# First layer's weighted sum: exponential steps waited for late, spread over all rows, and a new split into sets

## The reference

```python
for hd in range(4):
    h = inputs * W[hd]
    logits = (h @ a[hd, :D])[src] + (h @ a[hd, D:])[dst]
    e = exp(leaky_relu(logits, 0.2))              # one weight per edge and head
    rowsum = segment_sum(e, src, num_segments=N)
    agg = segment_sum(e[:, None] * h[dst], src, num_segments=N)
    outs.append(elu(agg / rowsum[:, None]))
return mean(outs)
```

## Time and profile before

| | us |
|---|---|
| median of 3 runs | 4653.99 |
| the three runs | 4649.1 to 4656.62 |
| span of the profiled execution | 4657.2 |
| the stretch of `sum_neighbours`, in the profile | about 1046 to 1733 |

### The profile page before, as it was taken

The page is one execution under the profiler, slowest core; times in us unless marked ns, Lnnn a source line. Parts: engine busy times, 40 slices in busy tenths (PEclk is TensorE's granted clock), DMA queues, the critical chain, the costliest instruction groups (busy, mean ns, idle before and its releaser), DMA issues. The chain is left out here.

```text
span 4657.2 us, 47765 instructions
## 1 busy us (share of the span) xinstructions
PE 1697.7 (36%) x10711; PEld 958.0 (21%) x10711; DVE 2833.9 (61%) x4928; ACT 1748.2 (38%) x4626; POOL 1878.2 (40%) x1844
## 2 busy tenths in 40 slices
PE   3162111100000000006666332322222179899989
PEld 2142111100000000001221110111111168444444
DVE  5837599873777779884554333657777757422131
ACT  1334311102565658335665433234444355010011
POOL 0044555556777720024555553277767340000000
PEclk6576555555555555555655666655555589999999
DMA  3000000016666620001222222277778445767845
GB/s 131 14 19 1 3 1 1 1 58 181 175 185 178 183 55 0 0 14 37 63 63 72 63 64 60 97 227 243 241 230 256 114 131 146 293 241 268 281 157 204
DMA packets 215391, 553.46 MB, mean 119 GB/s; under 512 B 46178, under 2 KB 112412, under 8 KB 214405
## 3 DMA queue, kind: packets, MB, share of 16 engines
q0 software_dynamic: 99984, 272.83, 20.7%
q1 hardware_dynamic: 115188, 278.18, 17.3%
HBM read 485.70 MB, written 65.20 MB: 118 GB/s over the span
## 5 line engine op out<-in xcount | busy, mean ns | idle before, releaser
L2829 PE MATMUL fourth_bank<-fourth_tile,fourth_z 128*128 128x512 f16 (+1 forms) x2800 | 559.6, 361 | 19.7 <-DVEq L2990 10.1
L1320 POOL DMA_INDIRECT blend_got<-rec,blend_slot x416 | 401.7, 966 | 365.7 <-DMA blend_got<-rec,blend_slot 252.0
L2191 POOL DMA_INDIRECT heads_got<-rec,heads_slot x416 | 467.6, 1124 | 185.4 <-issue 123.6
L1724 POOL DMA_INDIRECT sum_got<-rec,sum_slot x416 | 451.9, 1086 | 164.9 <-issue 127.5
L1044 POOL DMA_INDIRECT table<-edges_record,edges_place x391 | 393.0, 1005 | 292.3 <-DMA table<-edges_record,edges_place 186.2
L258 PE MATMUL blend_count<-blend_mov,blend_stat 128*128 x980 | 366.7, 473 | 326.8 <-DVE blend_mov L1372 180.0
L214 PE MATMUL edges_p_key<-kept_ident,edges_key_row 128*128 128x128 f32 x4 | 1.1, 428 | 1024.8 <-DVEq L176 1024.8
L1798 DVE TENSOR_TENSOR first_y<-first_y,sum_got 128x516 f32 x416 | 290.8, 699 | 126.5 <-issue 33.5
L1372 DVE TENSOR_SCALAR blend_mov<-built_iota_low,built_low 128x800 f16 x490 | 217.0, 444 | 210.6 <-issue 103.9
L2829 PEld LDWEIGHTS fourth_bank<-fourth_tile,fourth_z 128*128 128x128 f16 x2800 | 261.6, 99 | 311.4 <-issue 14.7
L2304 DVE TENSOR_TENSOR third_a_y<-third_a_y,heads_got 128x520 f32 x416 | 287.8, 692 | 55.9 <-issue 41.5
(11 more groups left out here) (675 smaller groups left out, 4471.1 us busy)
## 6 DMA issues: line engine op xcount, KB each, us to landing
fourth_tile<-cs SPq DMA_DIRECT2D x100, 800.0 KB, 4.5
fourth_tile<-ct SPq DMA_DIRECT2D x100, 800.0 KB, 4.3
ct<-blend_cst SPq DMA_DIRECT2D x20, 1000.0 KB
heads_counts<-ct SPq DMA_DIRECT2D x25, 800.0 KB
cs<-heads_flipped SPq DMA_DIRECT2D x25, 800.0 KB
attend_cnt<-ct SPq DMA_DIRECT2D x50, 256.0 KB
sort_low_wide<-low SPq DMA_DIRECT2D x4, 3136.0 KB
attend_cnt<-ct SPq DMA_DIRECT2D x25, 288.0 KB
```

What stands on the lines that cost most here:

```text
L1320: pool.indirect_dma_start(got[:, buf, r, :], None, rec_dram, bass.IndirectOffsetOnAxis(ap=slot[:, t:t + 1], axis=0)).then_inc(gathered[t % ...
L1724: pool.indirect_dma_start(got[:, t % (HELD * PART), :], None, rec_dram, bass.IndirectOffsetOnAxis(ap=slot[:, t:t + 1], axis=0)).then_inc(g ...
L2191: pool.indirect_dma_start(got[:, buf, r, :], None, rec_dram, bass.IndirectOffsetOnAxis(ap=slot[:, t:t + 1], axis=0)).then_inc(gathered[buf ...
L2829: last = pe.matmul(bank[m][:, 0:w], z2[s % 2][:, k, part, :], tile[:, n % RING, at:at + w], start=(k == 0 and part == 0), stop=(k == NB - ...
```

## The change

- `Trail` stands in for `Chain` in the weighing. A step is issued without a wait behind it; the wait for it comes just ahead of the next step (`advance` calls `settle`, then takes the step), so an add into `y` that stands between two steps doesn't wait for the first.
- The steps are spread over all rows of a set: after row r, as many as bring the count to 38(r + 1) // rows. In a set of 32 rows that is one or two after each row, from the first row on; in one of 16 rows two or three.
- At the start of a part the order is now: wait for the last step, multiply the first head, load the registers, wait for the multiplication.
- The sets are 2, 2, eleven times 4, 2 and 2 parts: 16 rows in the first two and last two sets, and 32 in the others, 15 sets in all. Tiles keep their size; a small set uses the front of them.
- `factors` is raised in a step of its own, after the step that writes the weights has been waited for.

POOL's code keeps its waits, and so does the buffer of eight parts. The core of the diff:

```diff
+class Trail:
+    def __call__(self, ins):
+        self.n += 1
+        ins.then_inc(self.sem, 1)
+    def settle(self):
+        if self.n:
+            self.eng.wait_ge(self.sem, self.n)
+    def advance(self, steps):
+        self.settle()
+        next(steps, None)
...
-    SETS, ROWS = 13, SLOT_ROWS // 13
-    PARTS = 4
-    PART = ROWS // PARTS
-    HELD = 8
+    PART, HELD = 8, 8
     ON_ACT = 3
-    FIRST_EXP = 12
+    STEPS = 38
+    parts_of = [2, 2] + [4] * 11 + [2, 2]
+    first_part = [sum(parts_of[:n]) for n in range(len(parts_of) + 1)]
+    SETS, MOST = len(parts_of), max(parts_of) * PART
...
-                for part in range(PARTS * n, PARTS * (n + 1)):
+                for part in range(first_part[n], first_part[n + 1]):
                     wait_gathered(dve, part)
-                    step(dve.tensor_tensor(logits, own[:, :, part * PART:(part + 1) * PART],
+                    trail(dve.tensor_tensor(logits, own[:, :, part * PART:(part + 1) * PART],
...
-                yield from exp_once(step, dve, l, live[:, at].unsqueeze(1).to_broadcast([P, heads, ROWS]), weights[n % 2], tmp)
+                yield from exp_once(trail, dve, l, live[:, at].unsqueeze(1).to_broadcast([P, heads, rows]), weights[n % 2][:, :, 0:rows], tmp)
+                yield
                 dve.sem_inc(factors, 1)
...
-            for _ in weigh(0):
-                pass
+            opening = weigh(0)
+            for _ in range(STEPS):
+                trail.advance(opening)
             for n in range(SETS):
+                rows = parts_of[n] * PART
                 exps = weigh(n + 1) if n + 1 < SETS else iter(())
-                for r in range(ROWS):
-                    t = n * ROWS + r
+                taken = 0
+                for r in range(rows):
+                    t = first_part[n] * PART + r
                     if r % PART == 0:
+                        trail.settle()
+                        weigh_first_head(n, t // PART)
                         dve.reg_load(regs, chunk_row[0:1, t:t + PART])
-                        weigh_first_head(PARTS * n + r // PART)
+                        trail.settle()
...
                     dve.tensor_tensor(sums, sums, got[:, t % (HELD * PART), 0:heads * F1], ALU.add).then_inc(added, 1)
-                    if r >= FIRST_EXP:
-                        next(exps, None)
-                        next(exps, None)
-                for _ in exps:
-                    pass
+                    while taken < STEPS * (r + 1) // rows:
+                        trail.advance(exps)
+                        taken += 1
```

More of the change, by code:

```diff
@@ L249, in __call__, with __init__ @@
         self.eng.wait_ge(self.sem, self.n)
+class Trail:
+    def __init__(self, eng, sem):
+        self.eng, self.sem, self.n = eng, sem, 0
+    def __call__(self, ins):
[7 more added lines that the diff above has]
+        next(steps, None)
 def clear(pe, K, bank, width):
@@ L1683, in sum_neighbours @@
     dst_f = spare[:, 8 * P:12 * P].rearrange("p (q l) -> p q l", q=4)
-    size = heads * ROWS
+    size = heads * MOST
     def tiles(flat, count):
-        return [flat[:, k * size:(k + 1) * size].rearrange("p (k r) -> p k r", r=ROWS) for k in range(count)]
+        return [flat[:, k * size:(k + 1) * size].rearrange("p (k r) -> p k r", r=MOST) for k in range(count)]
     kept_tiles = tiles(K["record"][:, :, :].rearrange("p a b -> p (a b)").bitcast(F32), 8) + tiles(K["place"][:, :].bitcast(F32), 3)
-    small, weights = kept_tiles[0:10], [kept_tiles[10], c.sb("weights", [P, heads, ROWS])[:, :, :]]
+    small, weights = kept_tiles[0:10], [kept_tiles[10], c.sb("weights", [P, heads, MOST])[:, :, :]]
     p_slot, p_reach, p_chunk = c.ps("p_slot"), c.ps("p_reach"), c.ps("p_chunk")
@@ L1694, in sum_neighbours @@
     loaded, v, turned, sought, ready = (c.sem(n) for n in ("loaded", "v", "turned", "sought", "ready"))
-    factors, weighed, added = c.sem("factors"), c.sem("weighed"), c.sem("added")
+    factors, weighed, added, trailed = c.sem("factors"), c.sem("weighed"), c.sem("added"), c.sem("trailed")
     gathered = [c.gather_sem(f"gathered{k}") for k in range(HELD)]
@@ L1715, in _ @@
             pool.wait_ge(ready, 1)
-            for part in range(PARTS * SETS):
+            for part in range(first_part[SETS]):
                 if part == HELD - 1:
@@ L1760, in _ @@
             regs = [dve.alloc_register(f"chunk{k}") for k in range(PART)]
+            trail = Trail(dve, trailed)
             def weigh(n):
-                l, *tmp = small
-                at = slice(n * ROWS, (n + 1) * ROWS)
-                for part in range(PARTS * n, PARTS * (n + 1)):
+                rows = parts_of[n] * PART
+                l, *tmp = (tile[:, :, 0:rows] for tile in small)
+                at = slice(first_part[n] * PART, first_part[n + 1] * PART)
+                for part in range(first_part[n], first_part[n + 1]):
@@ L1767, in weigh @@
                     wait_gathered(dve, part)
-                    logits = l[:, :, part % PARTS * PART:(part % PARTS + 1) * PART]
-                    step(dve.tensor_tensor(logits, own[:, :, part * PART:(part + 1) * PART],
-                                           got[:, rows_of(part), heads * F1:RECORD].rearrange("p r k -> p k r"), ALU.add))
+                    logits = l[:, :, (part - first_part[n]) * PART:(part - first_part[n] + 1) * PART]
+                    trail(dve.tensor_tensor(logits, own[:, :, part * PART:(part + 1) * PART],
+                                            got[:, rows_of(part), heads * F1:RECORD].rearrange("p r k -> p k r"), ALU.add))
@@ L1771, in weigh @@
                     yield
-                step(dve.scalar_tensor_tensor(l, l, 0.2, l, ALU.mult, ALU.max))
+                trail(dve.scalar_tensor_tensor(l, l, 0.2, l, ALU.mult, ALU.max))
                 yield
-                yield from exp_once(step, dve, l, live[:, at].unsqueeze(1).to_broadcast([P, heads, ROWS]), weights[n % 2], tmp)
+                yield from exp_once(trail, dve, l, live[:, at].unsqueeze(1).to_broadcast([P, heads, rows]), weights[n % 2][:, :, 0:rows], tmp)
+                yield
@@ L1775, in weigh, with weigh_first_head @@
                 dve.sem_inc(factors, 1)
[L1777 to L1781, removed]
-            for _ in weigh(0):
-                pass
+            def weigh_first_head(n, part):
+                rows, r = got[:, rows_of(part), 0:rest * F1], (part - first_part[n]) * PART
+                e = weights[n % 2][:, 0, r:r + PART]
+                trail(dve.tensor_tensor(rows, rows, e.unsqueeze(2).to_broadcast([P, PART, rest * F1]), ALU.mult))
@@ L1809, in _ @@
                 act.wait_ge(factors, n + 1)
-                for r in range(ROWS):
+                for r in range(parts_of[n] * PART):
+                    t = first_part[n] * PART + r
                     if r % PART == 0:
-                        wait_gathered(act, PARTS * n + r // PART)
+                        wait_gathered(act, t // PART)
                     for k in range(rest, heads):
-                        part = got[:, (n * ROWS + r) % (HELD * PART), k * F1:(k + 1) * F1]
+                        part = got[:, t % (HELD * PART), k * F1:(k + 1) * F1]
                         last = act.activation(part, part, ACT.Copy, scale=weights[half][:, k, r:r + 1])
```

## The result

The changed kernel takes **4690.98 us**, median of four runs (4688.74 to 4699.54), against 4651.55 for the kernel before beside it (4647.31 to 4656.62): the ratio is 1.0073, with an interval of 1.0054 to 1.0092. That is 39 us, or 0.7%, slower. The profiled execution spans 4690.8, 33.6 more than before. The forecast was 4673, with a range of 4626 to 4712.

The account below looks back on a forecast made before the run. DVE was taken to set the pace, POOL within 2 us a set. Opening to 1182, nine cycles of 51.4 and 107 at the end gave 1751.6, 19 us slower than 1733.0: 4673, range 4626 to 4712.

Parts of the forecast that it names:

- the stop: In each large set, DVE waits at the fourth logits for the next set's gather; POOL waits some 7 us for adds.
- its own case: The forecast's main outcome for the whole kernel: a time of 4663 to 4688, chance 0.42.
- DVE's own work: DVE alone in a large set: 0.91 a row with one step, sum 37.1 us, 9.4 less than before.
- 13.0: Earliest time in us after a large set's start at which its fourth logits can run; DVE reaches them after about 5.2.
- part f + 7: Part read by the fourth logits, f being the set's first; its gathers wait for the previous set's last add.
- The cycle: From one fourth logits to the next in large sets: 8.2 + 31.1 + 12.1 = 51.4 us, against 46.5 before.
- The opening and the end: Stage's ends: first steady fourth logits at about 1182; from the last of them to the stage's end 107 us.
- the rival of the slow spell: The opening's 1.40 us a step comes again at 1105; at most 20 us reach the end: 4693, chance 0.10.
- The rival of gathers at full speed: DVE's long stops let every gather through at 1.25: cycle 47.0, 27 us faster, 4627, chance 0.15.
- No stop: Fourth logits find their gather landed and only POOL's pace binds: 60 us faster, 4594, chance 0.04.
- a draw: Gather period 1.30 to 1.39, cycle 48.2 to 50.2, ends cancel the stops: within 9.3 us of now, chance 0.18.
- The rule weighed there: Skill's rule that DVE locks out GpSimd's descriptor writes only in 2-port mode, so an fp32 two-tensor add holds no gather.

Follow-up runs that it names:

- adding it alone: Kernel before with only the steps spread over all 32 rows, each still waited for at once: 4723.81 us, ratio 1.0208.
- taking it out in two ways: Kernel after with equal sets and no steps in the first twelve rows: 4521.82 us; kernel after with POOL's gate row by row: 4524.43; unchanged kernel after: 4585.54.
- the second trace of the kernel after: Kernel after, unchanged, run again on a machine without slow spells, beside the kernel before: 4585.54 us, ratio 1.0061.
- the second trace of before: Kernel before, unchanged, run again on another machine, without slow spells: 4558.48 us.

## Why the prediction was right, and where its sizes were off

The direction and its cause were right: the stop, shown by adding it alone (ratio 1.0208) and by taking it out in two ways on one machine (64 and 61 us). That the time fell inside the range was partly luck. 39 us slower is twice the 19 forecast and lies outside the 4663 to 4688 that the forecast gave its own case; without spells the change costs 27 us (4585.54 against 4558.32).

- **DVE's own work** came as computed: 0.91 for a row with a step (1204.55 to 1205.46), and from the fourth logits to the next set's first add 34.2 in the second trace of the kernel after (1620.69 to 1654.90), against 37.1 - 5.2 + 1.5 = 33.4. The waits of the multiplication for a step before it are gone there: 0.2 us over all 52, against 17.2 in the second trace of before. Adds next to gathers take up to 0.77 instead of 0.70 there.
- **The stop** is where it was put: in every large set of the second trace, and in the first for POOL in every one, for DVE only in four, as said above. But the reason that I gave for its start holds for few sets. I counted 13.0 from the set's first add, because the last add of the set before opens the gate. That is so at 1183.77, where the gate opened 2.3 earlier (1180.80 + 0.70) and the logits ran 11.1 behind the set's start (1194.87). In the second trace they ran 15.8 to 16.9 behind it, and 19.9 in the first large set. There the gate was open, and POOL was still busy with the part before: in the set at 1353.38 it came to the first gather of part f + 7 only at 1365.79 - 7 x 1.25 = 1357.0, 3.6 into the set. What holds POOL back is its own stop in the set before, at part f + 4. The sum for the cycle, which counts from that stop, carries this; the 13.0 doesn't.
- **The cycle** was put at 51.4 and is 50.5 in the kernel after (fourth logits at 1194.9 and 1649.4, nine cycles) and 50.2 in its second trace (1168.6 and 1620.7). In that second trace the pieces, as means of the nine, are 4.2 to POOL's restart (4.3 predicted), 42.1 for 31 periods (43.2), 3.9 to the logits (3.9). The mis-sized term is the gather's period beside a running DVE: if the stops' 9.7 periods cost 1.25, it comes to (42.1 - 12.1) / 21.3 = 1.41, where I took 1.46 from a span of two-step rows.
- **The opening and the end** held without spells: from the first gather to the first steady fourth logits 126.5 (127.3 predicted; but my own terms, 125 and 3.9, make that 129, and I wrote 1182 where they give 1184), from the last of them to the stage's end 107.9 (107). The sum for the stage was 696.9 and the second trace has 686.5, the 10.4 being nine times 1.2 of the cycle.
- **With spells** the terms that failed are those two. In the kernel after they are 140.8 and 120.0, 13 us more each, and the cycles take 8.1 less than forecast. So the stage ends 17.8 later than the forecast's 1751.6. That is the rival of the slow spell, with 20 us and 4693: its mechanism was real on the machine of the first comparison, and I gave it 0.10 and put it only in the opening. In the cycles between, the spell hid under the stop, where DVE would have waited anyway. It struck at the end as much: 1649.4 to the next set's first add at 1690.0 took 40.6 for 33.4, and the last set of 32 took 42.0 for 36, while the two small sets took 21.9 and 15.5, as forecast.
- **Two errors set off each other.** The trace of before held a spell too; its stage is 15.5 us longer than that of the second trace of before, which has none. Without spells on either side my sum would have meant 696.9 - 662.8 = 34 slower, and the difference there is 23.7.
- The rival of gathers at full speed fell: the mean gather in the stops' presence is 1.02 to 1.04, not 0.95. No stop and a draw fell as well, the draw narrowly: it had cycles of 48.2 to 50.2 (by my own sum 48.0 to 49.9), and 50.2 and 50.5 were measured. The rule weighed there isn't the whole truth either: a gather is held under an add of two fp32 tensors, as below.

**What stays open** is the cause of the spell. What the runs show in this stage is: one instruction in 1.40 us on ACT, after 22 at the usual pace (seen twice), and steps 1.40 apart on DVE; it starts while gathers are issued back to back; it is there with and without the change; it was in every trace taken where before took 4626 or more, and in none where it took 4562 or less. That the gathers delay the fetching of the other engines' instructions is only argued, and every kernel here issues gathers, so nothing separates the two. Open too is how much of the 72.4 us behind this stage is the same thing.

## What to carry to other kernels

Before spreading an engine's side work evenly, look at what each piece reads: a piece that waits for a transfer of the *next* block, moved to the front of this one, stops every instruction behind it and, through the buffer's gate, the transfers themselves. Move the independent steps and leave the waiting ones late, or release the buffer in the units in which it is filled. Taking the wait from behind a step, with the register load behind the multiplication, was worth 0.8% here by itself, and the spreading around it cost more than that, so parts of a change should be timed alone, and beside their baseline on the same machine.

## What the runs showed of the hardware

The spell of one instruction in 1.40 us, above, was not expected to reach past the opening; the fall of `L1825 <- issue` from 93.6 on one machine to 1.5 on another, for the same kernel, was the surprise.

The other is how a gather and a DVE instruction share. Timeline of the kernel after in its second trace, DVE and then POOL:

```profile
1376.58 0.76 DVE L1825 TENSOR_TENSOR first_y<-first_y,sum_got 128x516 f32 x1
...
1377.55 0.70 DVE L1825 TENSOR_TENSOR first_y<-first_y,sum_got 128x516 f32 x1
```

```profile
1376.61 0.95 POOL L1743 DMA_INDIRECT sum_got<-rec,sum_slot  x1 [0.30 <-issue]
1377.87 1.20 POOL L1743 DMA_INDIRECT sum_got<-rec,sum_slot  x1 [0.30 <-issue]
```

The gather at 1377.87 starts 0.32 into an add and ends 0.82 after that add does, as in rows 5. The one at 1376.61 starts 0.03 after the start of an add and isn't held: it takes its 0.95, and the add is stretched to 0.76. So here a gather that starts with an add lets the add pay 0.06, and one that starts inside it pays 0.25 itself. The whole trace agrees: all 52 adds that take over 0.72 have a gather starting within 0.05 of their own start, and the 74 gathers that start 0.05 to 0.4 into an add take 1.20 to 1.47 and end 0.81 to 0.83 behind it. The Trainium skill (SBUF — State Buffer, § SBUF: two separate sides) says that a DVE instruction with two SBUF inputs shares a port pair with a GpSimd operation that reads SBUF, and that whichever starts first holds it for its whole instruction while the other is fully blocked. The held gather agrees with that; the add of 0.76 beside a gather of 0.95 that overlaps nearly all of it doesn't, since it was not blocked for the gather's length.
